# Two orders of the same steps: a decoder block whose engine programs are woven from three lists

## What is computed

```
x = _layernorm(x + _L0_attn_ref(x, ...))                 # causal self-attention, 16 heads of 8, rope
x = _layernorm(x + _L0_xattn_ref(x, ctx, ...))           # cross-attention, layer norm of q and k per head
x = _layernorm(x + _L0_ffn_ref(x, ...))                  # gated FFN, 352 wide, FP4 blockwise quantization
x = _layernorm(x + _L1_attn_ref(x, ...))                 # linear attention with convolutions, MLP 512 wide
x = _layernorm(x + _L1_xattn_ref(ctx, x, ...))           # causal cross-attention over the context
x = _layernorm(x + _L1_ffn_ref(x, ...))                  # top-2 of 8 experts, 256 wide, silu-gated
```

## Time and profile before

| | us |
|---|---|
| median of 3 runs | 738.24 (737.21 to 739.14) |
| span of the profiled execution | 763.1 |
| PE busy | 568.6 (75%) |
| DVE busy | 531.9 (70%) |
| ACT busy | 327.7 (43%) |
| POOL busy | 200.5 (26%) |

### The profile page before, as it was taken

The page is one execution under the profiler, slowest core; times in us unless marked ns, Lnnn a source line. Parts: engine busy times, 40 slices in busy tenths (PEclk is TensorE's granted clock), DMA queues, the critical chain, the costliest instruction groups (busy, mean ns, idle before and its releaser), DMA issues.

```text
span 763.1 us, 13948 instructions
## 1 busy us (share of the span) xinstructions
PE 568.6 (75%) x4890; PEld 393.2 (52%) x4890; DVE 531.9 (70%) x1520; ACT 327.7 (43%) x642; POOL 200.5 (26%) x312
## 2 busy tenths in 40 slices
PE   5787668756788688775975784667886987679984
PEld 2466546534455347442764463444542675567861
DVE  9667677888667667673686778996855767455633
ACT  2653445312474465142634451126744632344632
POOL 2204201201203502046043011121024034454543
PEclk9897669667699989687888797777997885599998
DMA  9993000000000000011000000000000001132215
GB/s 276 326 298 98 28 1 2 1 0 0 2 1 0 1 1 3 1 33 54 2 6 0 1 2 1 0 2 0 2 0 1 2 1 40 58 96 68 78 54 155
DMA packets 45556, 32.34 MB, mean 42 GB/s; under 512 B 4281, under 2 KB 43457, under 8 KB 45361
## 3 DMA queue, kind: packets, MB, share of 16 engines
q1 hardware_dynamic: 41104, 25.49, 12.1%
q0 software_dynamic: 2272, 4.92, 1.9%
q10 hardware_dynamic: 2112, 1.05, 0.5%
HBM read 13.83 MB, written 17.62 MB: 41 GB/s over the span
## 4 chain that ended last, share of the span: by engine, by line
PE 43%; DVE 32%; ACT 11%; issue 7%; POOL 4%; another core or an unknown queue 2%; DMA 1%; DVEq 0%; ACTq 0%; POOLq 0%
PE ps L643 5%; PE ps L984 5%; PE ps L624 5%; PE ps L687 5%; DVE s_row_max L1408 2%; PE ps L998 2%; ACT s_probs L1135 2%; DVE s_probs L1413 2%; DVE s_r L1377 2%; PE ps L655 2%; PE ps L906 1%; PE ps L911 1%; DVE s_st L1380 1%; DVE s_work L1367 1%
## 5 line engine op out<-in xcount | busy, mean ns | idle before, releaser
L1954 POOL TENSOR_TENSOR s_rs<-s_mv,eps 128x1 f32<-128x1 f32 x80 | 17.1, 215 | 349.3 <-DVE s_mv L1383 349.2
L1408 DVE TENSOR_REDUCE s_row_max<-ps 128x16 f32<-128x1024 f32 x48 | 58.7, 1222 | 62.3 <-PE ps L643 47.2
L1115 ACT ACTIVATE s_pT<-ps 128x512 f32<-128x512 f32 x96 | 55.5, 594 | 56.6 <-PE ps L624 44.2
L624 PE MATMUL ps<-tabs,s_probs 128*128 128x128 f32 x384 | 64.2, 302 | 19.8 <-ACT s_probs L1135 12.2
L643 PE MATMUL ps<-s_k,s_q 64*64 64x256 f32 x768 | 64.8, 451 | 13.5 <-ACT s_q L1085 9.9
L624 PEld LDWEIGHTS ps<-tabs,s_probs 128*128 128x128 f32 x384 | 45.8, 152 | 40.7 <-issue 19.9
L1135 ACT ACTIVATE s_probs<-s_probs 128x1024 f32<-128x1024 f32 x48 | 50.6, 1055 | 24.0 <-DVE s_probs L1413 23.7
L1413 DVE TENSOR_TENSOR s_probs<-ps,s_row_max 128x1024 f32<-128x1024 f32 x48 | 58.7, 1222 | 1.3
L687 PE MATMUL ps<-s_v,s_pT 128*64 128x18 f32 x1536 | 54.9, 216 | 3.5 <-issue 1.4
L687 PEld LDWEIGHTS ps<-s_v,s_pT 128*64 128x64 f32 x1536 | 51.0, 143 | 12.0 <-issue 11.0
L984 PE MATMUL ps<-s_pT,s_k 128*128 128x128 f32 x312 | 48.4, 304 | 3.8 <-issue 1.6
(11 more groups left out here) (288 smaller groups left out, 1247.8 us busy)
## 6 DMA issues: line engine op xcount, KB each, us to landing
rows_io<-zero_rows SPq DMA_DIRECT2D x9, 1152.0 KB, 11.9
s_probs<-rows_io SPq DMA_DIRECT2D x39, 72.0 KB
s_xin<-in_x SPq DMA_DIRECT2D x4, 256.0 KB, 4.1
s_cin<-in_ctx SPq DMA_DIRECT2D x4, 256.0 KB, 4.1
wgu<-in_wg SPq DMA_DIRECT2D x1, 1024.0 KB
wgu<-in_wu SPq DMA_DIRECT2D x1, 1024.0 KB
wo<-in_wo SPq DMA_DIRECT2D x1, 1024.0 KB
out_x<-s_work SPq DMA_DIRECT2D x4, 256.0 KB, 2.3
```

The source lines that it names most:

```text
L624: ins = pe.transpose(h.ps[:, 2, tile(j)], h.probs[:, t % 2, 8 * part + 2 * j:8 * part + 2 * j + 2, :] .rearrange("p h k -> p (h k)"), ident)
L1115: act.activation(h.pT[:, t % 2, 4 * part:4 * part + 4, :].rearrange("p j q -> p (j q)"), h.ps[:, 2, :], ACT.Copy).then_inc(h.pT_here.sem, 1)
L1408: dve.tensor_reduce(h.row_max[:, t % 2, :], s3, AX, ALU.max).then_inc(h.max_here.sem, 1)
```

## The change

The four tables of `ORDER` are replaced by four others. Nothing else is changed: the steps, their instructions, their waits and the buffers are the same, and so is SP's queue. The table is six lines longer, so a line of the changed kernel has a number that is higher by 6.

```diff
 ORDER = {
     "pe": (
-        0, 1, 0, 2, 1, 0, 2, 2, 0, 1, 1, 0, 1, 1, 0, 3, 3, 0, 2, 1, 0, 2, 1, 0, 2, 1, 0, 1, 1, 0, 3, 1, 0,
...
+        2, 2, 0, 2, 2, 0, 1, 1, 0, 1, 1, 0, 2, 1, 0, 1, 1, 0, 1, 1, 0, 3, 2, 0, 1, 1, 0, 3, 1, 0, 1, 1, 0, 1,
...
     "act": (
...
     "dve": (
...
     "pool": (
...
```

## The result

| | before | after |
|---|---|---|
| median | 738.69 us (737.21 to 740.17, 4 runs) | 756.42 us (755.69 to 757.49, 4 runs) |
| ratio | | 1.0266, 95% interval 1.0225 to 1.0307 |
| span of the profiled execution | 763.1 | 754.7 |

The new order is slower by 2.7%, 18 us. The prediction said 737.0, in a range from 725 to 749: the sign is wrong and the time is outside. In the tables the medians are over all runs, and the ratios leave out the runs counted as slow, more than 1.5% above the fastest of their kernel (three of e5_pool_sends, two of e10_tail_full, one each of four others, and four of the 130 of before).

A forecast was written before the change was run, and what follows sets the result against it. No single engine was taken as the bound: PE and DVE hand work to and fro. −0.4 −3.2 (streams) +2.4 (experts' start) +0 (POOL) = −1.2 took 738.2 to 737.0 us, range 725 to 749.

The forecast's parts named there:

- What bounds the kernel: Whole kernel: no single bound, PE busy 75% and DVE 70%; a new order changes only waits, not instruction lengths.
- The stops: Waits of 11.6 and 5.3 us during POOL's sends, taken as mostly the profiled execution's own, seven chances in ten.
- The profile forecast of 754 to 760: Span expected for the changed kernel's profiled execution, against 763.1 us before.
- Part 1: Both streams up to about 627 us: exchanges gain 0.4 and 3.2 us, between −8.5 and +6.
- Rows 4: Second self-attention: DVE idled 1.31 us and PE 1.09 us; filling these gains at most 2.4 us.
- Place 1: DVE's 3.33 us wait for B's queries: B's last normalisation starts earlier, −0.4 us; A's early subtraction helps nobody.
- Part 2: Start of the experts: PE waits for B's shares and B's bias mix moves later, +2.4 us, between 0 and +4.
- slower: Rival, 744 us: at the experts' start B's transposes hold up PE, +4, with streams at +2; chance 0.27.
- 730: Rival: every swap letting a ready step go first counts, streams −8.5 and experts' start 0; chance 0.25.
- 733: Rival: the stops during POOL's sends occur in ordinary runs too, and the second shortens, −5 us; chance 0.10.
- Part 3: POOL's sends at the experts, 1.27 us apart: nothing waited for moves, 0, at worst one send, 1.3 us.
- The clock: PE's clock is 0.50 from 627 to 665 us; an earlier rise could save some 2 us, left out of the sum.

The follow-up runs named there:

- e5_pool_sends: The old order with only POOL's order from about 626 us on new; 741.04 us, ratio 1.0043.
- e10_tail_full: The old order to 626 us, then the new order on PE, ACT and DVE with POOL's sends in another, mended order; 738.00 us, ratio 0.9977.
- the five pieces: Five kernels, each the old order with one stretch new: 0 to 86, 86 to 160, 160 to 361, 361 to 409, 409 to 626 us; 735.68 to 744.00 us.
- the copy: The old order run and profiled again, with no edit that reaches a queue; 739.96 us, ratio 1.0008, profiled span 738.3 us.
- e8: The old order with only 361 to 409 us, the second turn's self-attention, in the new order; 743.04 us, ratio 1.0058.
- r4: The old order with the new order on all four engines only from about 626 us on; 741.08 us, ratio 1.0057.
- the mend: POOL's last sends reordered (eight of A, two of B, then two outputs per send): 738.00 us with only the end new, 752.22 with the whole new order.

## Why the prediction was wrong, point by point

- **What bounds the kernel** held: no single engine, and work handed to and fro. Between the two profiles PE's idle time moved and its busy time did not. But "a new order cannot shorten an instruction" hid the other side: it can lengthen one. The convolutions above take mostly 1.06 us each for 0.59, by the clock, and a normalisation takes 1.27 for 0.34, beside POOL. The prediction had no term for that.
- **The stops** were that one execution's, as I had taken with 0.7. The profile forecast of 754 to 760 came out (754.7) for a reason of its own: I had counted stops that were gone, and not the 16 us of waits that came. That is luck.
- **Part 1, the streams, −3.6: the step that failed.** I valued exchanges as fillers of idle time seen in the old trace, and counted "as many exchanged the wrong way round" as a balance. Measured, the five pieces cost −0.24 +0.72 +0.72 +0.58 +0.60 = +2.38%, or 17.6 us, and the whole is 13.0 us behind the copy at 625 us; the term had −3.6 with an upper bound of +6. The old order's trace shows the gaps that could be filled and hides the many places where the steps now stand right, which an exchange can only lose. The bound was made from the few waits of one trace; it should have come from how many ready steps could stand behind one that isn't. Such places show as waits of over 3 us (3.19, 3.31, 3.43 above), but a wait isn't its price: the old order waits 2.77 us round the first, and taking 2.0 us of the third away brought 0.7 to 1.0 us locally. Where the five pieces lose is shown; how much of it comes from such places and how much from the clock is read in two of them (160 to 361 and 361 to 409 us) and stays open in the others.
- **Rows 4** were the place of a gain of up to 2.4. The stretch round them is e8's, and it costs 0.58%, 4.3 us, in its trace most of it by the clock.
- **Place 1, −0.4**, was wrong in a way that the trace of after shows. VectorE's last normalisation now runs beside a residual that POOL makes, which stood elsewhere in the old order (VectorE, POOL, TensorE):

```profile
587.43 1.27 DVE L1395 TENSOR_SCALAR s_x<-s_r,s_mv,s_rs 128x128 f32<-128x128 f32 x1 [0.71 <-POOL s_rs L1963]
```

```profile
587.36 1.26 POOL L1980 TENSOR_TENSOR s_resid<-s_x,bo 128x512 f32<-128x512 f32 x1
```

```profile
588.76 0.47 PE L609 MATMUL ps<-tabs,s_x 128*128 128x128 f32 x1 [1.51 <-DVE s_x L1395]
```

  It takes 1.27 us for 0.34 and ends when POOL's operation ends (588.70 and 588.62). The wait of PE is 1.51 us for 0.91. The same pair has the same length in all seven traces with 409 to 626 us new and in none of the others at this place, so it belongs to the order. That A's subtraction comes early for nobody held.
- **Part 2, +2.4 by PE's wait for B's shares**: not seen. PE in after:

```profile
648.31 0.48 PE L982 MATMUL ps<-tabs,s_probs 128*128 128x128 f32 x1 [0.73 <-DMA s_probs<-rows_io]
648.58 1.92 PE L990 MATMUL ps<-s_pT,s_k 128*128 128x128 f32 x8
650.28 1.06 PE L968 MATMUL ps<-tabs,s_work 128*8 128x128 f32 x4
651.14 0.42 PE L982 MATMUL ps<-tabs,s_probs 128*128 128x128 f32 x1
```

  Block 0's `gate_up` starts 3.3 us behind its `weigh` (645.27), since the second of the two `turn`s ahead of it waits for its rows by DMA; I had given the two no wait. B's shares were written at 649.73 (0.19), before it ended: no gap. The rival *slower* (744) rested on the same gap and falls with it, though its sign came true. The two faster rivals, 730 and 733, fall too. The steps of that sum are off from their own terms by up to 0.2 us (647.1, 1.02 and 0.2 are 648.3, and block 2 would follow at 652.4), which changes nothing.
- **Part 3, POOL, 0 and at worst 1.3: the other step that failed.** I checked who needs a send and not what stands behind a send that waits. The earlier trace rows held 0.96 us and 0.30 ahead of it, and the prediction itself the distance of 1.27. 16 sends and 15 outputs at that pitch are 39 us in which TensorE gets to about block 15, so a pause in the row has no cover. The end cost +0.57% (4.2 us) in r4, and the mend gave 3.1 us there and 4.2 in the whole by the medians, about 2 in the traces, at a place that I had priced at nothing, at worst 1.3.
- **The clock** is 0.50 from 640 to 650 us and 0.92 from 650 to 660 in after, and 0.88 and 1.00 in the copy, which is 12 us further on in its steps. So it rises at about the same step, and the 2 us that an earlier rise would have given did not come.

## What to carry to other kernels

In a fixed order of in-order queues an exchange is worth what stands ready behind a step that waits. Go over the new order for steps that will wait with ready work behind them, on every engine, and count those, not the old trace's gaps. A queue that is rarely busy on the whole, as POOL with 27%, can set the pace for 40 us; compare its work in a stretch with that of the others before pricing a move in it at nothing. Take a second profile of the old kernel before explaining any one, and at a per cent don't trust one execution: two of the same order lay 8 us apart at one point.

## What the hardware showed

- An order alone moves TensorE's granted clock within a stretch: from 361 to 409 us it was 0.76 to 0.80 in five traces of the new order and 0.85 to 0.93 in fifteen of the old, and the stretch 4 to 5 us longer. The mean over a whole execution stays between 0.834 and 0.858 in all that were profiled. An execution moves it too: two of the same order had 0.59 and 0.83 in the same 20 us of their spans, and the matmuls of the additions at the end took 5.4 us in six traces and 3.8 in fourteen.
- A VectorE `tensor_scalar` from SBUF to SBUF of 0.34 us took 1.27 beside a POOL `tensor_tensor` of 1.26. The Trainium skill's page "SBUF — State Buffer", section "Who interferes with whom", says that a VectorE operation in a mode with two ports, which `tensor_scalar` can enter, and GpSimd contend for a shared pair of ports, and that the one which comes second is blocked for the other's whole instruction. This trace agrees: POOL's began 0.07 us earlier, and VectorE's ended 0.08 us behind it. Which mode VectorE's was in no run shows.
- Indirect sends by POOL follow each other at 1.27 us, 0.96 busy and 0.30 for issue, tokens of 144 columns and outputs of 128 alike; some take 1.0 to 1.2 us.
